# The second layer of the first expert stage as three products of operands split into two rounded f32 parts

## The reference

```
def _L0_ffn_ref(hidden_states, router_w, router_b, w1, w2):
    b, s, d = hidden_states.shape            # 1, 2048, 256; 8 experts, 1024 hidden
    x = hidden_states.reshape(-1, d)
    route = jax.nn.softmax(x @ router_w + router_b, axis=1)
    max_prob = jnp.max(route, axis=1, keepdims=True)
    max_ind = jnp.argmax(route, axis=1)
    out = jnp.zeros_like(x)
    for e in range(num_experts):
        a, g = jnp.split(x @ w1[e], 2, axis=1)
        y = jax.nn.silu(a) * g @ w2[e]
        out = jnp.where((max_ind == e)[:, None], y, out)
    return (out * max_prob).reshape(b, s, d)
...
x = x + tanh(g_xattn[0]) * L0_xattn(layernorm(x), ctx)
x = x + tanh(g_ffn[0])   * L0_ffn(layernorm(x))
x = x + tanh(g_xattn[1]) * L1_xattn(ctx, layernorm(x))
x = x + tanh(g_ffn[1])   * L1_ffn(layernorm(x))
```

## Time and profile before

| | |
|---|---|
| median of 3 runs | 1289.95 us |
| the runs | 1284.48, 1289.95, 1294.92 us |
| span of the profiled execution | 1292.1 us |
| PE busy | 1154.9 us, 89% of the span |
| DVE, ACT, POOL busy | 528.1, 463.6, 481.8 us |
| first expert stage, first and last record of L413 and L429 | 117.2 us to 379.0 us |

### The profile page before, as it was taken

One profiled execution on the slowest core, in us unless ns is written; L12 is line 12 of the kernel. 1 busy time (PEld: TensorE's weight loads), 2 busy tenths in 40 slices (PEclk: granted clock), 3 DMA queues, 4 the chain that ended last, 5 costly groups with the idle time before them and its releaser, 6 DMA issues.

```text
span 1292.1 us, 19235 instructions
## 1 busy us (share of the span) xinstructions
PE 1154.9 (89%) x7062; PEld 852.0 (66%) x7062; DVE 528.1 (41%) x1283; ACT 463.6 (36%) x1067; POOL 481.8 (37%) x499
## 2 busy tenths in 40 slices
PE   4965999999978799999999999999948999999895
PEld 3765999999965444554555555434438888898895
DVE  5675222221119876675767667512070000010010
ACT  4111222221101455655555555663303333333331
POOL 1151111111103476666767657660002333333231
PEclk9856999999997899999999999999958999999998
DMA  6154878778841000000000000003007999999994
GB/s 214 61 172 178 299 284 301 282 302 317 312 155 55 1 1 1 1 18 1 1 17 1 1 1 18 21 30 135 0 1 261 303 315 293 310 313 292 295 292 124
DMA packets 48504, 193.10 MB, mean 149 GB/s; under 512 B 7930, under 2 KB 28796, under 8 KB 32412
## 3 DMA queue, kind: packets, MB, share of 16 engines
q1 hardware_dynamic: 35886, 170.93, 36.9%
q0 software_dynamic: 10464, 18.36, 6.2%
q10 hardware_dynamic: 2062, 2.60, 0.6%
HBM read 175.48 MB, written 16.38 MB: 148 GB/s over the span
## 4 chain that ended last, share of the span: by engine, by line
PE 63%; DMA 17%; DVE 9%; issue 5%; ACT 3%; POOL 2%; SPq 0%; POOLq 0%; ACTq 0%; DVEq 0%
PE PQ L413 16%; DMA out<-Z,SI 14%; PE PB L429 9%; PE PB L523 8%; PE PQ L508 7%; PE PB L490 5%; PE PQ L563 4%; PE PB L513 4%; DVE Z L928 4%; PE PB L291 3%; PE PQ L490 2%; DMA Z<-xn,SI 2%; DMA V<-in_ctx 1%; PE PQ L291 1%; PE PB L322 1%
## 5 line engine op out<-in xcount | busy, mean ns | idle before, releaser
L413 PEld LDWEIGHTS PQ<-Z,WS 128*128 128x128 f32 x2720 | 323.2, 193 | 21.8 <-issue 15.4
L413 PE MATMUL PQ<-Z,WS 128*128 128x128 f32 x2720 | 327.8, 277 | 10.6 <-issue 9.6
L429 PE MATMUL PB<-WS,Z 128*128 128x256 f32 x992 | 234.3, 380 | 0.0
L928 DVE TENSOR_REDUCE Z<-PB 128x1 f32<-128x402 f32 x319 | 172.2, 568 | 73.5 <-PE PB L490 72.2
L429 PEld LDWEIGHTS PB<-WS,Z 128*128 128x128 f32 x992 | 179.2, 191 | 19.2
L508 PE MATMUL PQ<-QS,KS 128*128 128x512 f32 x416 | 173.7, 433 | 3.3 <-ACT Z L1144 2.0
L1082 ACT ACTIVATE Z<-PQ,WS 128x128 f32<-128x128 f32 x312 | 88.9, 367 | 199.2 <-PE PQ L413 199.2
L508 PEld LDWEIGHTS PQ<-QS,KS 128*128 128x128 f32 x416 | 77.1, 189 | 103.0 <-issue 67.6
L1144 ACT ACTIVATE WS<-PQ 128x512 f32<-128x512 f32 x208 | 109.6, 604 | 83.7 <-PE PQ L508 83.7
L1144 ACT ACTIVATE Z<-PQ 128x512 f32<-128x512 f32 x208 | 109.8, 603 | 78.8 <-PE PQ L508 78.7
L1215 POOL DMA_INDIRECT out<-Z,SI x39 | 61.9, 1587 | 200.2 <-DMA out<-Z,SI 168.7
(11 more groups left out here) (240 smaller groups left out, 1209.7 us busy)
## 6 DMA issues: line engine op xcount, KB each, us to landing
WS<-in_w SPq DMA_DIRECT2D x62, 1024.0 KB, 6.5
WS<-in_w SPq DMA_DIRECT2D x23, 2048.0 KB, 8.0
WS<-in_w SPq DMA_DIRECT2D x39, 1028.0 KB, 7.0
xn<-WS SPq DMA_DIRECT2D x32, 128.0 KB, 1.8
X<-in_x SPq DMA_DIRECT2D x4, 512.0 KB, 10.3
WS<-yd SPq DMA_DIRECT2D x4, 512.0 KB, 5.6
out<-X SPq DMA_DIRECT2D x4, 512.0 KB, 2.9
dep_d<-Z SPq DMA_DIRECT2D x13, 128.0 KB, 1.7
```

What stands on the lines that cost most here:

```text
L413: t = e.matmul(bank[:, j * P:j * P + P], w[:, k, o:o + P], FXT[i % 2][:, k * P:k * P + P], start=k == 0, stop=k == 1)
L429: t = e.matmul(y, FS[c % 4][:, j * P:j * P + P], w[:, 4 * n + j, :], start=n == 0 and j == 0, stop=n == 1 and j == 3)
L928: e.tensor_reduce(MP[j % 2][:, i:i + 1], PB[bank_of["pc", r]][:, 0:PIECE], AX.X, ALU.max).then_inc(v_pc, 1)
```

## The change

In the first expert stage, each operand of the second layer is split into a rounded part and the rest, both f32r: h = HH + HL, w2 = WH + WL. The product is HH*WH + HH*WL + HL*WH; HL*WL is left out. The rounded part of a half's w2 is made by ACT (`w2_high`, a copy of 1024 columns), the rest by DVE (`w2_low`, a subtraction of 1024 columns), side by side as [high | low] in `W2P`, two buffers that lie in `QS`. h is split by DVE alone: a copy into `HH` and a subtraction into `HL`, which lie in `AU`, one buffer each. `down(c)` then has for each of its four j one f32r matmul with 512 columns, HH by [WH | WL], and one with 256 columns, HL by WH. High and low products of HH land in the two halves of the PSUM bank, and `out_row` adds them with a second DVE instruction.

New waits: HH of half c is written only when `down(c - 1)` is through; `w2_high(c)` when `down(c - 2)` is through; `load_down(i)` waits for `w2_low` (v_wl) in place of `down` (t_down). The constant columns of `AU` are filled by POOL behind the second `queries` step of the attention, no more at the start.

```diff
--- before.py
+++ after.py
@@ -90,9 +90,11 @@
         V = sb("V", [P, NK * D]).rearrange("p (c d) -> p c d", d=D)
         Z0 = sb("Z0", [P, 4096])
         Z1 = sb("Z1", [P, 4096])
-        QS = [sb(f"QS{i}", [P, 2048], F32R).rearrange("p (h q) -> p h q", h=4) for i in range(2)]
+        QF = [sb(f"QS{i}", [P, 2048], F32R) for i in range(2)]
+        QS = [v.rearrange("p (h q) -> p h q", h=4) for v in QF]
         AK = [sb(f"AK{i}", [P, 1024], F32R).rearrange("p (h c) -> p h c", h=8) for i in range(2)]
-        AU = [sb(f"AU{i}", [P, 512], F32R).rearrange("p (h c) -> p h c", h=4) for i in range(2)]
+        AF = [sb(f"AU{i}", [P, 512], F32R) for i in range(2)]
+        AU = [v.rearrange("p (h c) -> p h c", h=4) for v in AF]
         MBH = sb("MBH", [P, 2 * NK], F32R)
         CT = sb("CT", [P, C_N])
         SM = sb("SM", [P, SMN])
@@ -152,6 +154,8 @@
         FXT = [Z0[:, 512 + 256 * i:768 + 256 * i] for i in range(2)]
         FS = [Z0[:, 1024 + 512 * i:1536 + 512 * i] for i in range(4)]
         FY = [Z0[:, 3072 + 256 * i:3328 + 256 * i] for i in range(2)]
+        W2P = [v.rearrange("p (j s n) -> p j s n", j=4, s=2) for v in QF]
+        HH, HL = AF
 
         B2 = X.rearrange("p c d -> p (c d)")[:, 0:E * D]
         RW1 = Z0[:, 0:2048].rearrange("p (k n) -> p k n", k=2)
@@ -202,6 +206,7 @@
         t_tr, a_tr, t_up, t_down, v_y = (
             [sem(f"{n}{l}") for l in range(2)] for n in ("t_tr", "a_tr", "t_up", "t_down", "v_y"))
         a_silu, v_h, a_h = sem("a_silu"), sem("v_h"), sem("a_h")
+        a_wh, v_wl, v_hh, v_hl, p_au = (sem(n) for n in ("a_wh", "v_wl", "v_hh", "v_hl", "p_au"))
 
         v_x2, v_qn, p_q, t_q, a_q, t_pc, v_pc, v_m, t_m, a_m = (
             sem(n) for n in ("v_x2", "v_qn", "p_q", "t_q", "a_q", "t_pc", "v_pc", "v_m", "t_m", "a_m"))
@@ -418,16 +423,29 @@
                     i, n = divmod(c, 2)
                     w = WS[i % 2][:, 4096:6144].rearrange("p (c n) -> p c n", c=8)
                     y = PB[6 + i % 2][:, 0:D]
-                    e.wait_ge((v_h, a_h)[l], c + 1)
+                    if l == 0:
+                        e.wait_ge(v_wl, c + 1)
+                        e.wait_ge(v_hl, c + 1)
+                    else:
+                        e.wait_ge(a_h, c + 1)
                     if n == 0:
-                        e.wait_ge(d_down[l][i % 2], landed(i, 2))
+                        if l == 1:
+                            e.wait_ge(d_down[l][i % 2], landed(i, 2))
                         if i == 0:
                             e.wait_ge(v_tab[l], 2)
                         if i >= 2:
                             e.wait_ge(v_y[l], i - 1)
                     for j in range(4):
-                        t = e.matmul(y, FS[c % 4][:, j * P:j * P + P], w[:, 4 * n + j, :],
-                                     start=n == 0 and j == 0, stop=n == 1 and j == 3)
+                        first, last = n == 0 and j == 0, n == 1 and j == 3
+                        if l == 1:
+                            t = e.matmul(y, FS[c % 4][:, j * P:j * P + P], w[:, 4 * n + j, :], start=first, stop=last)
+                            continue
+                        if not first:
+                            e.matmul(y, HL[:, j * P:j * P + P], W2P[n][:, j, 0, :], start=False, stop=False)
+                        t = e.matmul(PB[6 + i % 2], HH[:, j * P:j * P + P], W2P[n][:, j, :, :].rearrange("p s n -> p (s n)"),
+                                     start=first, stop=last)
+                        if first:
+                            t = e.matmul(y, HL[:, j * P:j * P + P], W2P[n][:, j, 0, :], start=False, stop=False)
                     t.then_inc(t_down[l], 1)
 
                 turn_x(0)
@@ -841,11 +859,23 @@
             e.wait_ge(v_flag, 3)
 
             def experts(l, nt, extra):
+                def w2_low(c):
+                    e.wait_ge(a_wh, c + 1)
+                    e.tensor_tensor(W2P[c % 2][:, :, 1, :], WS[c // 2 % 2][:, 4096 + 1024 * (c % 2):5120 + 1024 * (c % 2)]
+                                    .rearrange("p (j n) -> p j n", j=4), W2P[c % 2][:, :, 0, :].bitcast(F32),
+                                    ALU.subtract).then_inc(v_wl, 1)
+
                 def gated(c):
                     h = FS[c % 4]
                     e.wait_ge(t_up[l], 2 * c + 2)
                     e.wait_ge(a_silu, c + 1)
                     e.tensor_tensor(h, h, PB[2 * (c % 2) + 1], ALU.mult).then_inc(v_h, 1)
+                    e.wait_ge(v_h, c + 1)
+                    if c:
+                        e.wait_ge(t_down[l], c)
+                    e.tensor_copy(HH, h).then_inc(v_hh, 1)
+                    e.wait_ge(v_hh, c + 1)
+                    e.tensor_tensor(HL, h, HH.bitcast(F32), ALU.subtract).then_inc(v_hl, 1)
 
                 def out_row(i):
                     y = PB[6 + i % 2][:, 0:D]
@@ -863,13 +893,16 @@
                     if i >= 2:
                         e.wait_ge(d_y[l][i % 2], landed(i - 2, 2))
                     if l == 0:
-                        e.tensor_scalar(FY[i % 2], y, tabp[:, i:i + 1], None, ALU.mult).then_inc(v_y[l], 1)
+                        vc.step(e, e.tensor_scalar(FY[i % 2], y, tabp[:, i:i + 1], None, ALU.mult))
+                        e.scalar_tensor_tensor(FY[i % 2], PB[6 + i % 2][:, D:2 * D], tabp[:, i:i + 1], FY[i % 2],
+                                               ALU.mult, ALU.add).then_inc(v_y[l], 1)
                     else:
                         vc.step(e, e.tensor_tensor(FY[i % 2], y, bias, ALU.add))
                         e.tensor_scalar(FY[i % 2], FY[i % 2], tabp[:, i:i + 1], None, ALU.mult).then_inc(v_y[l], 1)
 
                 for c in range(2 * nt + 1):
                     if c < 2 * nt and l == 0:
+                        w2_low(c)
                         gated(c)
                     if c >= 2 and c % 2 == 0:
                         out_row((c - 2) // 2)
@@ -881,7 +914,7 @@
                     a = AK[k % 2]
                     k3 = CK[:, k, :].rearrange("p (h d) -> p h d", h=E)
                     if k == 0:
-                        e.wait_ge(p_set, 16)
+                        e.wait_ge(p_set, 8)
                     if k >= 2:
                         e.wait_ge(t_tr[0], bank_of["kt", k - 2, 1])
                     e.tensor_copy(a[:, :, 0:32], k3).then_inc(vc.sem, 1)
@@ -907,6 +940,8 @@
 
             def split(j):
                 au = AU[j % 2]
+                if j == 0:
+                    e.wait_ge(p_au, 8)
                 mp = MP[j % 2].rearrange("p (h s) -> p h s", s=4)
                 e.wait_ge(v_pc, 16 * j + 16)
                 if j >= 2:
@@ -1073,7 +1108,7 @@
                     i, n = divmod(c, 2)
                     e.wait_ge(t_up[l], 2 * c + 1 if l == 0 else c + 1)
                     if c >= 4:
-                        e.wait_ge(t_down[l], c - 3)
+                        e.wait_ge((v_hl, t_down[1])[l], c - 3)
                     if l == 0:
                         e.activation(FS[c % 4], PB[2 * (c % 2)], ACT.Silu).then_inc(a_silu, 1)
                     else:
@@ -1083,8 +1118,18 @@
                                              bias=WS[i % 2][:, o:o + 1])
                         t.then_inc(a_h, 1)
 
+                def w2_high(c):
+                    if c % 2 == 0:
+                        e.wait_ge(d_down[l][c // 2 % 2], landed(c // 2, 2))
+                    if c >= 2:
+                        e.wait_ge(t_down[l], c - 1)
+                    e.activation(W2P[c % 2][:, :, 0, :], WS[c // 2 % 2][:, 4096 + 1024 * (c % 2):5120 + 1024 * (c % 2)]
+                                 .rearrange("p (j n) -> p j n", j=4), ACT.Copy).then_inc(a_wh, 1)
+
                 turn_x(0)
                 for c in range(2 * nt + 1):
+                    if c < 2 * nt and l == 0:
+                        w2_high(c)
                     if c < 2 * nt:
                         gated(c)
                     if c % 2 == 0 and c // 2 + 1 < nt:
@@ -1170,14 +1215,9 @@
         def _(e):
             e.memset(zero, 0.0).then_inc(p_set, 1)
             e.memset(nh, -0.5).then_inc(p_set, 1)
-            for t in AK + AU:
+            for t in AK:
                 e.memset(t[:, :, 96:128].bitcast(F32), 0.0).then_inc(p_set, 1)
-            for t in AU:
-                e.memset(t[:, :, 0:96].bitcast(F32), 0.0).then_inc(p_set, 1)
-            e.wait_ge(p_set, 8)
-            for t in AU:
-                e.memset(t[:, :, 96:97].bitcast(F32), 1.0).then_inc(p_set, 1)
-                e.memset(t[:, :, 98:99].bitcast(F32), 1.0).then_inc(p_set, 1)
+            e.wait_ge(p_set, 4)
             for t in AK:
                 e.memset(t[:, :, 97:98].bitcast(F32), -1.0).then_inc(p_set, 1)
                 e.memset(t[:, :, 99:100].bitcast(F32), -1.0).then_inc(p_set, 1)
@@ -1249,10 +1289,22 @@
                 pc.step(e, e.tensor_copy(a[:, 0:4, 0:32], q3))
                 e.tensor_tensor(a[:, 0:4, 32:64], q3, a[:, 0:4, 0:32].bitcast(F32), ALU.subtract).then_inc(p_q, 1)
 
+            def constant_rows():
```

(15 more changed lines are left out.)

## The result

| | before | changed |
|---|---|---|
| median | 1289.97 us (4 runs, 1284.48 to 1294.92) | 1277.05 us (4 runs, 1276.61 to 1277.59) |
| ratio | | 0.9898, 95% interval 0.9867 to 0.993 |
| span of the profiled execution | 1292.1 us | 1275.4 us |
| first expert stage, first `up` to last scaled row | 262.27 us | 250.40 us |

What follows compares the result with a forecast made beforehand. PE's instruction list was taken to bound the first expert stage: 19.2 us gained in `down` minus 1.9 us at the stage's end is 17.3 us, giving a median of 1272.7 us, range 1268 to 1283.

Steps and rivals of the forecast that it cites:

- PE's list bounds the stage, and what leaves it is gained: First expert stage: PE busy 30.00 of 30.00 us, never kept waiting; shortening its list was to gain 19.2 us.
- One column per cycle, 256 columns as fast per column as 512: New `down`: f32r moves one column per cycle of 2.4 GHz, so 0.216 us for 512 columns, 0.112 for 256.
- Rival 2: `down`: 256 f32r columns take two cycles per column, a half stays 1.73 us, time 1292 us; chance 8%.
- The weight load hides under 256 columns, with nothing to spare: `down`: loading 128 x 128 weights takes 0.107 us at full clock, just what 256 columns take, so it hides.
- Rival 1: `down`: weight load not hidden under 256 columns, a half 1.62 us, gain only 3 us, time 1287; chance 7%.
- Rival 4: `down`: bare weight load before each f32r matmul, a half 2.13 us, loss 20 us, time 1310; chance 1%.
- The choice of the surcharge: `down`: time added per f32r matmul taken near zero, at most 0.017 us; a half 1.31 us, bounds 1.28 and 1.42.
- The end of the stage: Last half: no `up` covers the split, PE idle about 1.4 us, second `out_row` instruction 0.5; cost 1.9 us once.
- VectorE under PE's tile: First expert stage: DVE work of 8.0 us fits in a 10.87 us tile with keys, 7.0 in 10.00 without.
- The transfers: w1 and w2 loads, issued together, fit: 341 GB/s needed against 411 seen, w1 needed after 11.3 us, 1.8 us of room.
- rival 3: Transfers in each tile: w1 lands after its 11.3 us limit and PE waits; 1308 us if at 13.5; chance 4%.
- The sum against the median: Whole kernel: 17.3 us off the span of 1292.1 gives 1274.8; span 2.15 over the median, so median 1272.7.

Runs made afterwards that it cites:

- Experiment 8: Changed kernel with the last tile's second layer in f32 on unsplit operands, one VectorE instruction for its output row: median 1273.51 us, stage 248.61 us.
- experiments 3 and 4: Changed kernel with the subtraction for w2's low part done twice: stage 249.41 us, tiles 11.04 and 10.19; three times: stage 288.32 us, tiles 12.67 and 11.79.
- Experiment 5: Changed kernel without the product of HL and the high part of w2, HL still made: stage 229.10 us, 21.3 us shorter.
- experiment 7: Changed kernel with w2's transfer waiting for `t_down`, as in the kernel before, in place of `w2_low`: stage 250.37 us, tiles 11.05 and 10.18.

## Why the prediction held, and where it was off

The forecast was a gain of 17.3 us, 1272.7; measured were 12.9, 1277.05. It lies in the range, on the forecast's side, and 1.0% is at the edge of what a measurement tells. The mechanism was right and one term of the sum too small; with the measured terms the sum is 46 x 0.32 - 2.2 = 12.5 us, and the 0.7 that the clock took from the first tile leave the 11.9 of the stage. Step by step:

- **PE's list bounds the stage, and what leaves it is gained: right.** PE is at 30 of 30 before and after, tiles shortened by exactly what `down` shortened, and experiment 2 with the old `down` and all the new vector work has the old tiles.
- **One column per cycle, 256 columns as fast per column as 512: right** (0.120 against 0.228). Rival 2 fell with it.
- **The weight load hides under 256 columns, with nothing to spare: right.** The floor seen at 128 columns, 0.112, is just under the 0.120 of 256 columns. Rival 1 would have needed 0.19 behind the short matmul. Rival 4 fell too: the rule of the Trainium skill that loads overlap only matmuls of another row group ("TensorE: Matmul & The Clock Gate", Part 3) does not hold in these runs, where each of 16 matmuls in a row brings its own weights for all rows and starts 0.228 behind the last.
- **The choice of the surcharge: the term that was mis-sized.** I took 0.003 to 0.005 us per f32r matmul from the f32 rows of the stage, since those have no waits inside a group like the new ones, and kept the 0.017 of the attention as the upper bound, which I put down to its waits. Series without any wait have 0.014, so at most 0.003 of it is theirs. The working was also off by itself: the rows shown in the earlier trace rows are 0.41 apart, which is (0.41 - 0.381) / 2 = 0.0145 per matmul and not 0.017 (that is the median of all 117 such pairs in the attention, 0.416 apart). Those rows give a half of 1.40, just what the tile shows. A half is 1.41 us by the tile, not 1.31 (the upper bound was 1.42), and 46 x 0.10 = 4.6 us of the gain were not there. That the time still fell into the range is due to this upper bound, which was kept for another reason. The row of the right kind of instruction was the better witness than the row of the right kind of place.
- **The end of the stage: 1.9 forecast, 2.17 measured** (5.66 - 4.13, and 0.64 by which the last two `down` are themselves shorter). The mechanism was right, PE idle 1.41 us and a second instruction (0.52). The rest is how the idle time is counted, from the end of a record at 363.35, where by the spacing the next matmul was due at 363.18, and the 0.07 more behind the first matmul of the group (364.75 to 364.94). Experiment 8 takes 1.5 us of it away.
- **VectorE under PE's tile: right,** 20.5 of 30 us (22 forecast). By experiments 3 and 4, 2.5 us per tile more are free and 5 are not.
- **The transfers: right, rival 3 did not come.** w1 lands after 8.1 us (limit 11.3). Experiment 5 gives the room, about 1 us per tile; experiment 7 shows that in the changed kernel the old wait of w2 would do as well.
- **The sum against the median.** I took 17.3 off both the span and the median. The span moved by 16.7, which looks like the forecast and is luck: 3.9 of it are the second expert stage, whose code is the same, and 0.8 the attention. The median moved by 12.9, near the 11.9 of the stage, but its interval of 9 to 17 us is wide; the tile lengths are what shows the gain.

## What to carry to other kernels

Where TensorE is busy without a gap, three f32r products of split operands beat one f32 product by 18% per matmul of 256 columns (1.41 against 1.73 us for four), as long as the splits fit under the other matmuls. They need about 5 us of VectorE's and 2 us of ScalarE's time per tile of 11 us, which must have a home. Price a kind of instruction by its own rows, wherever in the program they stand: the surcharge of 0.014 us per f32r matmul was in the trace of before, and I explained it away by where it was seen. Compare tiles, not stages or spans, when the gain is 1%: the rise of the clock alone moved the stage by up to 1.2 us. Last, look at the last round of a pipelined loop: what was hidden in all others is bare there, and it can be given the old form.
